# Cross-attention on one core: context, W_audio and the keys' projection ahead of the text weights' Gram matrix; the keys' mean, variance and inverse root earlier

## What is computed

```
text_p  = x @ W_text + b_text            # 512 -> 512
audio_p = ctx @ W_audio + b_audio        # 384 -> 512
Q = layer_norm(text_p, g1, beta1);  K = layer_norm(audio_p, g2, beta2);  V = audio_p
alpha = softmax(Q @ K.T / sqrt(512))
out = layer_norm(alpha @ V @ W_out + b_out + x, g_out, beta_out)
```

## Time and profile before

| | us |
|---|---|
| median of 3 runs | 272.67 (272.31 to 272.85) |
| the profiled execution | 268.94 |
| its span on the core | 267.2 |
| TensorE busy in the span | 253.9 (95%) |
| VectorE, ScalarE, GpSimd busy | 233.4, 206.7, 206.8 |
| the prologue, to the first `project` | about 48.8 |
| one step of the loop once it is full | about 6.4 |

### The profile page before, as it was taken

The page is one execution under the profiler, slowest core; times in us unless marked ns, Lnnn a source line. Parts: engine busy times, 40 slices in busy tenths (PEclk is TensorE's granted clock), DMA queues, the critical chain, the costliest instruction groups (busy, mean ns, idle before and its releaser), DMA issues.

```text
span 267.2 us, 5945 instructions
## 1 busy us (share of the span) xinstructions
PE 253.9 (95%) x1667; PEld 232.3 (87%) x1667; DVE 233.4 (87%) x712; ACT 206.7 (77%) x517; POOL 206.8 (77%) x238
## 2 busy tenths in 40 slices
PE   7799999999999999999999999999999999999970
PEld 6678878989999999999999999999999999999620
DVE  3868479889999999999999999999999999999874
ACT  4776258235788889989988898889989988999870
POOL 7076540011189999999999999999999999999994
PEclk9999999999999999999999999999999999999996
DMA  6916099442225454444554555454444444542127
GB/s 201 293 52 196 12 324 382 119 128 74 80 85 172 162 172 159 161 160 167 172 180 175 173 163 178 158 168 157 157 159 158 157 162 157 180 166 82 78 117 275
DMA packets 19312, 43.25 MB, mean 162 GB/s; under 512 B 2034, under 2 KB 2366, under 8 KB 19290
## 3 DMA queue, kind: packets, MB, share of 16 engines
q1 hardware_dynamic: 18666, 41.96, 46.5%
q10 hardware_dynamic: 624, 1.06, 1.3%
HBM read 21.19 MB, written 16.78 MB: 142 GB/s over the span
## 4 chain that ended last, share of the span: by engine, by line
PE 71%; POOL 12%; DMA 6%; DVE 5%; ACT 2%; issue 1%; SPq 1%; POOLq 0%; DVEq 0%
PE psY L1326 23%; PE psY L1337 11%; PE psT L1255 9%; PE psO L1349 9%; PE psY L1330 3%; DMA xs<-in_x_dram 3%; POOL zs L457 3%; POOL zs L463 3%; DMA zs<-in_ctx_dram 3%; PE psE L1305 2%; PE psE L1306 2%; PE psY L1147 2%; POOL rstd L485 2%; POOL rstd L469 2%; POOL zs L510 2%
## 5 line engine op out<-in xcount | busy, mean ns | idle before, releaser
L1326 PE MATMUL psY<-proj,x_hi 128*128 128x336 f32 x512 | 103.1, 323 | 0.0
L1326 PEld LDWEIGHTS psY<-proj,x_hi 128*128 128x128 f32 x512 | 82.7, 189 | 5.5 <-issue 0.4
L457 POOL TENSOR_TENSOR zs<-zs,gain 128x512 f32<-128x512 f32 x54 | 68.7, 1294 | 0.0
L463 POOL TENSOR_TENSOR zs<-zs,shift 128x512 f32<-128x512 f32 x54 | 68.6, 1293 | 0.0
L469 POOL TENSOR_TENSOR rstd<-stat_eps,neg_half 128x4 f32<-128x4 f32 x30 | 30.4, 1014 | 37.5 <-DVE stat_eps L990 35.8
L1337 PE MATMUL psY<-proj,x_lo 128*128 128x336 f32 (+1 forms) x256 | 50.6, 320 | 0.0
L978 DVE CUSTOM_DVE_ANT_0 waste_dve<-psY,xs,sums 128x515 bf16<-128x515 f32 x64 | 48.4, 756 | 2.3
L678 ACT ACTIVATE zs<-hid,shift,rstd 128x512 f32<-128x512 f32 x58 | 47.1, 813 | 0.0
L998 DVE SCALAR_TENSOR_TENSOR hid<-psO,inv_sum,xs 128x512 f32<-128x512 f32 x60 | 44.8, 747 | 1.9 <-PE psO L1349 0.6
L636 ACT ACTIVATE x_hi<-psT 128x512 fp32r<-128x512 f32 x64 | 38.2, 596 | 8.9 <-PE psT L1255 7.0
L876 DVE TENSOR_TENSOR x_lo<-psT,x_hi 128x512 fp32r<-128x512 f32 x64 | 43.7, 682 | 0.6 <-ACT x_hi L636 0.6
(11 more groups left out here) (264 smaller groups left out, 420.5 us busy)
## 6 DMA issues: line engine op xcount, KB each, us to landing
xs<-in_x_dram SPq DMA_DIRECT2D x64, 256.0 KB, 3.0
out_dram<-zs SPq DMA_DIRECT2D x30, 512.0 KB, 2.8
proj<-proj SPq DMA_DIRECT2D x4, 768.0 KB, 9.1
xs<-in_L_xattn_W_text_dram SPq DMA_DIRECT2D x4, 256.0 KB, 3.5
xs<-in_L_xattn_W_out_dram SPq DMA_DIRECT2D x2, 512.0 KB, 4.4
out_dram<-zs SPq DMA_DIRECT2D x4, 256.0 KB, 2.2
wa<-in_L_xattn_W_audio_dram SPq DMA_DIRECT2D x1, 768.0 KB, 6.9
zs<-in_ctx_dram SPq DMA_DIRECT2D x1, 462.0 KB
```

What stands on the lines that cost most here:

```text
L457: nc.gpsimd.tensor_tensor(zs[:, q, t, :], zs[:, q, t, :], gain[:], ALU.mult).then_inc(zg_ready, 1)
L463: nc.gpsimd.tensor_tensor(zs[:, q, t, :], zs[:, q, t, :], shift[:], ALU.add).then_inc(out_ready, 1)
L1326: nc.tensor.matmul(psY[:, t, to:to + HALF], x_hi[:, par, t, k * P:(k + 1) * P], proj[:, q, k, right * HALF:(right + 1) * HALF], start=(k = ...
```

## The change

What the diff does, by engine:

- SP: the context is issued first, then W_audio and W_text by quarters in turn, with no waits between; W_out follows at once. The waits ahead of x keep their counts on `lin_ready`.
- TensorE: `keep_busy` runs 10 instead of 8 matmuls, on a constant that GpSimd now sets first. Context turns, the first nine of the twelve audio products and the vectors' turn stand ahead of `text_transposes`, the last three ahead of `gram(0)`. The keys' mean stands in the middle of `gram(1)`. The variance's three matmuls and `key_scales` stand ahead of the rest of the values; `turn` stands behind `values_product(1)`.
- VectorE: the sums of squares (now three of them here and one on ScalarE), the root's preparation and the centring of b_text stand ahead of the `lo` parts of W_text. `linear(0)` stands behind the keys' `lo` parts, `linear(1)` behind `diag_lo`, `linear(2)` behind `value(1)`, `linear(3)` behind `value(2)`.
- GpSimd: `krstd` ahead of the four `triangle`; four more memsets, for buffers that are now read at full height.
- ScalarE: context first, `t_hi` and `key_square` interleaved with the halves of W_out.

The diff, cut to its core:

```diff
@@ SP
-            for k in range(KD):
-                sp.dma_start(wt[:, k, :], wt_rows[:, k, :]).then_inc(wt_loaded[k], 16)
             sp.dma_start(cx, ctx.rearrange("b s d -> s b d")).then_inc(ctx_loaded, 16)
-            sp.wait_ge(wt_loaded[1], 16)
-            sp.dma_start(wa[:], w_audio.rearrange("(k p) h -> p k h", p=P)).then_inc(wa_loaded, 16)
+            load_audio(0)
+            load_text(0)
+            load_audio(1)
+            load_text(1)
+            load_text(2)
+            load_audio(2)
+            load_text(3)
@@ POOL
+            pool.wait_ge(kvar_ready, 1)
+            nc.gpsimd.tensor_tensor(krstd[:, 0:3], kvar[:, 0:3], neg_half[:, 0:3], ALU.pow).then_inc(krstd_ready, 1)
             triangle(0)
...
-            pool.wait_ge(kvar_ready, 1)
-            nc.gpsimd.tensor_tensor(krstd[:, 0:3], kvar[:, 0:3], neg_half[:, 0:3], ALU.pow).then_inc(krstd_ready, 1)
@@ DVE
+            gram_dot(1)
+            gram_dot(2)
+            gram_dot(3)
...
+            text_lo(0)
+            dve.wait_ge(root_ready, 1)
+            nc.vector.tensor_copy(root_cols[:], root[:]).then_inc(root_cols_ready, 1)
+            text_lo(1)
...
-            for k in range(KH):
-                keys_lo(k)
-                if k < 2:
-                    linear(k)
-            linear(2)
...
-            linear(KD - 1)
             dve.wait_ge(krstd_ready, 1)
...
+            linear(1)
...
             lo_part(0, 0, 0)
             value(1)
+            linear(2)
             value(2)
+            linear(KD - 1)
@@ PE
+            pe.wait_ge(ksqsum_ready, KH - 1)
...
+            last.then_inc(kvar_psum, 1)
             pe.wait_ge(g_lo, 1)
             values_product(0)
...
+            key_scales()
+            pe.wait_ge(g_lo, 2)
+            values_product(1)
             for j in range(KD):
                 turn(j)
-            pe.wait_ge(g_lo, 2)
-            values_product(1)
-            key_scales()
             pe.wait_ge(kvar_ready, 1)
             values_product(2)
```

More of the change, by code:

```diff
@@ L574, in _ @@
             gram_square(0)
+            text_sum(1, 3)
+            act.wait_ge(vec_ready, 1)
+            audio(0)
             for k in range(KH):
@@ new lines, in _ @@
+            dve.wait_ge(mean_psum, 1)
+            dve.wait_ge(vT_ready, KH)
+            for k in range(KH):
+                nc.vector.tensor_tensor(kT[:, k, :], vT[:, k, :], A_BANK[0][:, 0:BS], ALU.subtract).then_inc(kc_ready, 1)
+            t_lo(0)
+            for k in range(1, KH):
+                dve.wait_ge(ksq_ready, k + 1)
+                if k > 1:
+                    dve.wait_ge(ksqsum_ready, k - 1)
+                nc.vector.tensor_tensor(kSqLive, kSq0 if k == 1 else kSqLive, KSQ[k], ALU.add).then_inc(ksqsum_ready, 1)
@@ new lines, in _ @@
+            t_lo(1)
+            link(nc.vector.memset(kvar[:], 1.0))
+            dve.wait_ge(kvar_psum, 1)
+            for n, (at, w) in enumerate(KEYS):
+                last = nc.vector.tensor_scalar(kvar[0:w, n:n + 1], A_BANK[1][0:w, n:n + 1], EPS, None, ALU.add)
+            last.then_inc(kvar_ready, 1)
+            t_lo(2)
+            t_lo(3)
+            dve.wait_ge(krstd_ready, 1)
+            for n, (at, w) in enumerate(KEYS):
+                nc.vector.tensor_scalar(diag_hi[:, at:at + w], ident[:, 0:w], krstd[:, n:n + 1], None, ALU.mult).then_inc(diag_ready, 1)
@@ L842, in _ @@
+            for n, (at, w) in enumerate(KEYS):
+                dve.wait_ge(diag_ready, n + 1)
+                nc.vector.scalar_tensor_tensor(diag_lo[:, at:at + w], ident[:, 0:w], krstd[:, n:n + 1],
+                                               f32(diag_hi[:, at:at + w]), ALU.mult, ALU.subtract).then_inc(diag_ready, 1)
+            linear(1)
             dve.wait_ge(vec_ready, 1)
@@ L879, in _ @@
[L879 to L882, removed]
-                dve.wait_ge(ksq_ready, k + 1)
-                if k > 1:
-                    dve.wait_ge(ksqsum_ready, k - 1)
-                nc.vector.tensor_tensor(kSqSum, kSq0 if k == 1 else kSqSum, KSQ[k], ALU.add).then_inc(ksqsum_ready, 1)
-            link(nc.vector.memset(kvar[:], 1.0))
@@ L888, in _ @@
-            for k in range(2, KD):
-                t_lo(k)
-            dve.wait_ge(kvar_psum, 1)
-            for n, (at, w) in enumerate(KEYS):
-                last = nc.vector.tensor_scalar(kvar[0:w, n:n + 1], A_BANK[1][0:w, n:n + 1], EPS, None, ALU.add)
-            last.then_inc(kvar_ready, 1)
-            linear(KD - 1)
-            dve.wait_ge(krstd_ready, 1)
-            for n, (at, w) in enumerate(KEYS):
-                nc.vector.tensor_scalar(diag_hi[0:w, at:at + w], ident[0:w, 0:w], krstd[0:w, n:n + 1], None, ALU.mult).then_inc(diag_ready, 1)
@@ L1135, in keep_busy @@
                 for n in range(count):
[L1136 removed]
+                    nc.tensor.matmul(bank[:, 0:P], mean_of, mean_of, start=True, stop=True)
             def text_transposes(j):
@@ L1143, in text_transposes, with audio_product @@
                         last.then_inc(wtT_psum, 1)
[L1145 to L1149, removed]
-            pe.wait_ge(ident_ready, 1)
-            keep_busy(8, psE)
+            def audio_product(j, k):
+                pe.wait_ge(wa_loaded[j], 16)
+                pe.wait_ge(cxT_ready, j + 1)
+                last = nc.tensor.matmul(V_BANK[k][:, 0:BS], wa[:, j, k * P:(k + 1) * P], cxT[:, j, :],
+                                        start=(j == 0), stop=(j == KA - 1))
+                if j == KA - 1:
+                    last.then_inc(vT_psum, 1)
+            pe.wait_ge(ones_ready, 1)
+            keep_busy(10, psE)
+            pe.wait_ge(ident_ready, 1)
+            pe.wait_ge(ctx_loaded, 16)
+            for k in range(KA):
+                for b in range(B):
+                    last = nc.tensor.transpose(CTX_BANK[k][:, b * S:(b + 1) * S], cx[:, b, k * P:(k + 1) * P], ident[0:S, 0:S])
+                last.then_inc(cxT_psum, 1)
+            for k in range(KH):
+                audio_product(0, k)
+            pe.wait_ge(vec_loaded, 16 * len(VECS))
+            nc.tensor.transpose(VEC_BANK[:, 0:len(VECS) * KH], vec_rows[:], ident[0:len(VECS) * KH, 0:len(VECS) * KH]).then_inc(vec_psum, 1)
+            for k in range(KH):
+                audio_product(1, k)
+            audio_product(2, 0)
+            pe.wait_ge(vec_ready, 1)
+            pe.wait_ge(cxT_ready, KA)
             text_transposes(0)
@@ L1203, in _ @@
             last.then_inc(mean_psum, 1)
-            pe.wait_ge(ones_ready, 2)
+            less_root(0)
+            gram(1, range(2, KH))
+            less_root(1)
             gram(2)
```

201 lines of the change are left out of this document (104 added, 97 removed).

## The result

| | before | after |
|---|---|---|
| median of 4 runs, us | 272.49 (271.31 to 272.85) | 280.12 (278.86 to 280.81) |
| the profiled execution, us | 268.94 | 278.86 |
| its mean granted clock | 0.990 | 0.976 |

The change makes the kernel slower: ratio 1.0386, 95% interval 1.0327 to 1.0446. Runs of the kernel before fall into two groups, near 268.5 and near 272.5 us, the second at a lower mean clock; the ratio goes by the faster runs and is therefore more than the quotient of the medians.

The account below looks back on a forecast made before the run. TensorE's own work was taken to bound the kernel. Copies 8.8 plus clock 2.0 made 10.8 us: 279.7 on the profiled execution's 268.94, 283.5 on the median 272.67; range 278.5 to 286.

Parts of the forecast that it names:

- rival (2): Copies land 15.0 us after the fourth `linear`, or SP delays x: 6.0 us late, 278.7 to 280.7; 22 in 100.
- The moved `linear`: Fourth `linear` on VectorE ends at 45.4 instead of 32.0, so SP's copies land at 63.2 and TensorE waits.
- The signs set down beforehand: SP's longest wait, for `lin`, ends at 45 to 46; TensorE waits 5 to 7 us before step 2; copies land 61 to 65.
- Its term, 8.8 us: Lateness of step 2 on TensorE: last copy lands at 63.2, wanted at 54.4.
- The bounds of 15.0 and 17.8: Time from the fourth `linear` to the copies' landing: 15.0 us for the bulk, 17.8 us for the last copy.
- The slips: Prologue delays: 0.4 us in the front, 0.5 before `key_scales`, 0.2 before the keys; 1.1 us together.
- the wait ahead of `key_scales`: TensorE waits 0.5 us for VectorE's diagonals, up to 1.3 if GpSimd is still at W_out's last halves.
- The clock: TensorE idles some 6 us before step 2, its clock falls, work behind begins at half rate: 2.0 us lost.
- The second queue: SP finishes copies at 52.7, places values for 17.2 us, then loads the next x: also 6.0 us late.
- Rival (1): Same wait for the copies before step 2, but TensorE's clock holds: 281.5 us; 18 in 100.
- Rival (3): Faster: TensorE loses its waits of 1.5 and 0.7 us and the copies land in time, 270.5 us; 3 in 100.
- rival (4): SP's order lets x or the copies pass, so the change doesn't do what it says; given no chance of its own.

Follow-up runs that it names:

- quick casts: The changed kernel, with VectorE stopped behind the fourth `linear` until GpSimd has finished the first Gram row: 277.3 us, ratio 1.0292.

## Why the prediction was right, point by point

The sign, the place and the chain from the late `linear` over SP's queue to the copies were right, and 280.12 lies in the range. It does not lie in the 282 to 286 of the forecast itself but in the 278.7 to 280.7 of rival (2), and the next x, which the forecast's sum leaves out, is what sets the end. Seven points.

- **The moved `linear`: right.** SP's longest wait behind the first x is for `lin`, the longest of TensorE is for the copies ahead of step 2, and both runs that moved `linear` alone show it to be necessary and sufficient. The signs set down beforehand came at the places named, mostly with smaller figures: the wait for `lin` ended at 43.7, TensorE's longest wait was 3.6 us, and the copies landed at 59.6.
- **Its term, 8.8 us, was 3.6 too large.** The fourth `linear` ended at 43.72 and not 45.4, and the copies took 15.9 us from there, not 17.8. The bounds of 15.0 and 17.8 held, and so they did with quick casts, where it was 61.21 - 44.19 = 17.0. The ceiling of 435 GB/s in the Trainium skill, "DMA: Bandwidth & Descriptors", Specifications, would have made it 10.9 (an estimate); the stretch from 56 to 58 moved 374 GB/s at a share of 1.05.
- **The slips were wrong in sign.** The front was to be 0.4 late and was 0.6 early: W_text's last quarter, issued at 4.2 and landed within 5.9, was there at about 10.1, not 11.1, and `gram(0)` waited 0.69 us, not 1 to 2.5. Then gram blocks, root rows and mean took 25.79 - 19.11 = 6.7 us, where it was 7.8 before. That hid a term that was too small, the wait ahead of `key_scales`: 1.25 instead of 0.5. The step behind the 0.5 took the diagonals' 1.6 us from the earlier trace rows, measured while GpSimd did little beside them; the change puts the triangles there, and they took 2.7.
- **The clock: right, 2.45 where 2.0 was said.** The clock falls in a wait of 3.6 us, shorter than the 6 foreseen. The 2.0 was partly luck: its 0.12 us a pass is half of 0.24, while the four in 0.63 of the earlier trace rows give 0.16 and, by the same sum, 1.3; and the half rate lasted 6.2 us, not 3.8. The Trainium skill, "TensorE: Matmul & The Clock Gate", "HAM oscillation — how this bites in real kernels", has the next piece start cold, and the trace agrees: step 2 ran at 0.50 from its start at 59.6 until 65.8, and at 1.00 for its last 2 us.
- **The second queue was only a rival, and it is what sets the end.** The step that failed is its price in rival (2): placements 17.2 us as in the earlier trace rows, x needed 6.0 us late, less than the copies' 8.8, so I let the copies decide. SP was through with the copies at 52.6, as priced (52.7): the fourth `linear` was 1.7 sooner, and the wait for GpSimd's small operations took that back. Behind the copies the placements took 20.8, and x landed at 76.8, 9.9 late. The copies' 5.2 and the clock's 2.45 add up to 7.7, and the wait for x adds the last 2.1. That the sum came within 0.9 us is luck: the term that was too large (8.8, by 3.6) and the one left out (2.1) nearly met. Rival (2), added to the profiled execution, gives 274.9 to 276.9 against the 278.86 measured; only on the median does it hit.
- **VectorE's own delay was left out.** Two `linear` among the values made TensorE wait 1.3 us for `vT_lo` and 1.0 for `proj`; with early `linear` both waits are gone. The wait for the copies covered them.
- **The step from the profiled execution to the median was wrong.** I added before's 3.7 us; for the changed kernel that difference is 1.3. Of the 3.4 us by which 283.5 was too high, 2.5 are this and 0.9 the sum (9.9 instead of 10.8).

Rival (1), the clock holds, fell with the stretches from 60 to 66. Rival (3), faster, and rival (4), the order lets x pass, fell with SP's waits. What stays open is why the placements took 20.8 us: no run took the copies away from in front of them. The whole excess lies in the first seven, 9.4 us (52.70 to 62.07) against 5.5 before; the other fourteen took 11.3 against 11.6. That the DMA engines were busy does not explain it by itself: before, the first two took 0.86 us each at a share of 1.06, and the slowest here, the first of this row with 2.41 us, ran at a share of 0.50.

```profile
58.27 3.10 SPq L361 DMA_DIRECT2D wo_hi<-wa  x2
```

## What to carry to other kernels

Before a small operation is moved to where its engine has time, follow its semaphore to the queue that waits on it, and then everything that stands behind that wait in the queue, down to the last transfer that someone needs. Where a queue has two consumers, work out both floors; the later one sets the end, and a gain ahead of it (a clock that holds, a faster engine) only makes the wait longer. A duration is good for a new order only if the neighbours are the same: ask which engine will now work beside it.

## What the runs showed of the hardware that I had not expected

- VectorE and GpSimd can slow each other, by factors, in some operations. With GpSimd's triangles beside them the diagonals took 1.27 and 1.43 us, without 0.63 and 0.78, while the triangles' operations took 0.45 to 0.50 either way; with VectorE at work beside them GpSimd's three operations took 1.07, 2.01 and 1.13 us, without 0.21, 0.21 and 0.23. Both were switched by one wait each. Not every neighbour does it: in the kernel with early `linear` GpSimd's three ran beside VectorE's `cd_parts` and a `zs` that reads PSUM, and took 0.21, 0.21 and 0.24 us; VectorE's `hid`, four of 128 x 308 that also read PSUM, took 1.86 us with triangles beside it (the two runs with triangles behind the diagonals) and without.
- The issue of a DMA can become slow: single placements took up to 2.41 us of SP's time behind the copies, and 21 of them 19.0 to 21.5 us in the kernels with late `linear`, where they took 17.2 before.
- The clock fell on the work behind waits as short as 2.9 us (two waits, 2.9 and 3.4, in the kernel before with late `linear`), and the work behind such a wait then ran at half rate for several us, in the changed kernel for 6.2 of step 2's 8.3 us. It made no difference whether the wait was for a transfer or for VectorE (`vT_lo`, 3.5 us).
